# Expert stages in parts of 12 and 4 token tiles, causal query blocks first to last, four operand steps inside the passes

## The reference, cut to what matters

```python
# small-head attention, 16 heads of 8; full in the first layer, causal in the second
q = q * cos + _rotate_half(q) * sin ; k = k * cos + _rotate_half(k) * sin
scores = einsum('bqhd,bkhd->bhqk', q, k) / sqrt(D) ; causal mask in layer 2
y = softmax(scores) @ v ; x = x + y @ proj_w
# experts: layer 1 has 8 experts, top 2, and a shared one; layer 2 has 4 experts, top 1
logits = h @ router_w
out += gate[:, e] * (silu(h @ w_gate[e]) * (h @ w_up[e])) @ w_down[e]
```

## Time and profile before

| | us |
|---|---|
| median of 3 runs | 2046.22 |
| the profiled execution's span | 2040.1 |
| what lies around the span | 6.1 |
| PE busy | 1822.2 |
| DVE busy | 1547.6 |
| ACT busy | 1380.9 |
| POOL busy | 415.4 |

### The profile page before, as it was taken

How to read it: one execution, slowest core, us unless ns; L and a number is a source line. 1 busy time by engine, 2 the same in 40 slices (tenths; PEclk the granted TensorE clock), 3 DMA queues, 4 the chain that set the end, 5 groups by cost and what they waited for, 6 DMA issues and landing times. The chain is left out here.

```text
span 2040.1 us, 39849 instructions
## 1 busy us (share of the span) xinstructions
PE 1822.2 (89%) x15560; PEld 907.5 (44%) x15560; DVE 1547.6 (76%) x2263; ACT 1380.9 (68%) x2565; POOL 415.4 (20%) x650
## 2 busy tenths in 40 slices
PE   6699999999999798489989999999778999999784
PEld 2122222222223388435667776767512322233384
DVE  5899999999997443446767777877578979886434
ACT  3499999999999643255645656566347898888331
POOL 4201000000002324323432121221330101123413
PEclk8699999999999998889999999999867999999598
DMA  5000000000000378400000000000100000000274
GB/s 168 1 3 3 5 10 4 5 9 5 8 7 7 107 264 284 124 0 1 1 1 1 1 1 1 1 1 1 53 1 2 5 3 12 5 12 6 60 262 154
DMA packets 52874, 81.51 MB, mean 40 GB/s; under 512 B 9200, under 2 KB 37744, under 8 KB 52560
## 3 DMA queue, kind: packets, MB, share of 16 engines
q1 hardware_dynamic: 47520, 70.50, 10.9%
q0 software_dynamic: 3072, 6.30, 1.0%
q10 hardware_dynamic: 2096, 2.17, 0.4%
HBM read 64.13 MB, written 12.06 MB: 37 GB/s over the span
## 5 line engine op out<-in xcount | busy, mean ns | idle before, releaser
L826 DVE TENSOR_REDUCE a_mx<-psum 128x2 f32<-128x1024 f32 (+2 forms) x832 | 906.1, 1156 | 73.2 <-PE psum L601 40.2
L752 ACT ACTIVATE a_cs<-psum 128x512 f32<-128x512 f32 (+3 forms) x1664 | 857.0, 572 | 80.7 <-PE psum L619 62.4
L642 PE MATMUL psum<-a_cs,a_V 128*16 128x256 f32 (+1 forms) x6400 | 501.7, 384 | 20.9 <-ACT a_OD L732 9.7
L601 PE MATMUL psum<-a_KS,a_QS 48*128 48x512 bf16 (+3 forms) x1664 | 324.9, 381 | 32.9 <-DVE a_mx L826 29.7
L619 PE MATMUL psum<-a_QS,a_KS 51*128 51x512 bf16 (+3 forms) x1664 | 336.6, 378 | 4.9 <-ACT a_cs L752 3.1
L2122 PE MATMUL psum<-b_VW,b_ST 128*128 128x129 f32 x2176 | 252.5, 277 | 13.3 <-DVE X L2232 13.3
L2122 PEld LDWEIGHTS psum<-b_VW,b_ST 128*128 128x128 f32 x2176 | 248.5, 194 | 15.0 <-DVE X L2232 15.0
L619 PEld LDWEIGHTS psum<-a_QS,a_KS 51*128 51x128 bf16 x1664 | 87.7, 93 | 355.0 <-ACT a_cs L752 310.3
L2103 PE MATMUL psum<-b_GT,AT 128*128 128x512 f32 (+3 forms) x640 | 242.9, 534 | 1.6 <-ACT b_ST L2158 1.6
L642 PEld LDWEIGHTS psum<-a_cs,a_V 128*16 128x16 f32 x6400 | 107.1, 94 | 244.7 <-issue 120.2
L2207 DVE TENSOR_TENSOR b_M<-b_M,b_ST 128x512 f32<-128x512 f32 (+3 forms) x288 | 174.8, 607 | 43.1 <-ACT b_ST L2158 12.6
(11 more groups left out here) (225 smaller groups left out, 1514.5 us busy)
## 6 DMA issues: line engine op xcount, KB each, us to landing
e_W<-in_l_experts SPq DMA_DIRECT2D x45, 576.0 KB, 5.5
e_W<-in_l_experts SPq DMA_DIRECT2D x21, 768.0 KB, 5.8
yg<-e_yout SPq DMA_DIRECT2D x14, 256.0 KB, 6.0
xg<-zeros SPq DMA_DIRECT2D x2, 1472.0 KB, 9.8
a_cs<-in_rope ACTq DMA_DIRECT2D x4, 512.0 KB, 9.5
a_QS<-a_mrow SPq DMA_DIRECT2D x128, 3.0 KB
a_cs<-in_rope SPq DMA_DIRECT2D x1, 2048.0 KB, 7.8
a_num<-a_OD SPq DMA_DIRECT2D x120, 16.0 KB
```

The source lines that it names most:

```text
L601: mm = pe.matmul(ps[:, 2 * slot + half, 0:width], QS[rows, 2 * p + i, q_cols(qb, qt * P, P)], KS[rows, 2 * p + i, c * BLK:c * BLK + width] ...
L642: mm = pe.matmul(ps[32 * j:32 * j + 2 * HD, AV_BANK, a:b], V[:, kt, HPP * p + j, :], probs(e, a, b), start=(kt == 0 and half == 0), stop=last,
L752: act.activation(probs(HPP * s + j, c, BLK), ps[:, plan.bank(entry), c:BLK], ACT.Exp, scale=scale).then_inc(exp_done, 1)
L826: dve.tensor_reduce(mx[:, pk % 2, qt, 2 * i:2 * i + 2, c], banks, AX.X, ALU.max).then_inc(max_done, 1)
```

## The change

In both expert layers the parts become 12 and 4 tiles: 31 and 15 slots in the first layer, 15 and 7 in the second. Three blocks are early in both. In the first layer 16 of part 0's 24 scatters stay in the attention block, in the second 4 of 12; half of the rest are issued first in the expert block, half after the power of the late block's norm. Blocks whose gathered results don't fit into part 1's slots are collected, measured and normalized behind the last slot (`uncollected`, `unmeasured`, `closing`).

In the causal attention the query blocks go 0, 1, 2, 3, and the operands in the order k0 q0 k1 q1 k2 q2 k3 q3. Four stay in the lead; k2, q2, k3, q3 begin at halves 20, 44, 80 and 112 of the passes (`begun`). There their placement goes by four pairs through the two-slot ring and VectorE makes all four copies; ROTATE, REST, LOW, HIGH, MIDDLE and PLACE are their offsets in halves. The lead keeps 19 maxima (45 before) and two turned rows (one before). The second half of the cos and sin table is loaded into other memory, since the first table's memory holds the exponentials.

```diff
-        self.operands = [("k", 0), ("q", order[0])] + [("k", n) for n in range(1, NB)] + [("q", n) for n in order[1:]]
+        self.operands = []
+        for qb in order:
+            fresh = [("k", n) for n in range(self.chunks(qb)) if ("k", n) not in self.operands]
+            self.operands += fresh[:1] + [("q", qb)] + fresh[1:]
+        self.leading = len(self.operands) - len(begun)
+        self.begun = {self.leading + i: u for i, u in enumerate(begun)}
...
+        for s, u in self.begun.items():
+            for j in range(2):
+                self.halves[u + j].append(("project", s, j))
+            for v in range(NU):
+                self.halves[u + self.PLACE + 2 * v].append(("place", s, v))
...
     def by_vector(self, s, v):
-        return s < EARLY and v % 2 == 1
+        return s >= self.leading or s < EARLY and v % 2 == 1
...
-                front.scatter(pool, 0)
+                front.scatter(pool, 0, 0, front.SENT_EARLY)
...
+                def place_pair(s, v):
+
+                    which = 0 if plan.operands[s][0] == "k" else 1
+                    slot = slot_of(("place", s, v))
+                    if v == 0:
+                        pe.wait_ge(low, s + 1)
+                    for t in range(TERMS):
+                        for i in (2 * (v % 2), 2 * (v % 2) + 1):
+                            rows = slice(32 * i, 32 * (i + 1))
+                            mm = pe.matmul(ps[:, 2 * slot + i % 2, :], place[rows, which, t, SETS[v // 2][i], :],
+                                           terms[rows, s % 2, t, :], start=(t == 0), stop=(t == TERMS - 1))
+                    mm.then_inc(max_ready, 1)
...
-        self.blocks = [sorted(order[n:n + 2]) for n in range(0, NB, 2)]
+        self.blocks = [sorted(order[:split]), sorted(order[split:])]
...
+        if split == 3 and top2:
+            self.WHEN = {"project": (1, 2, 3), "turn": (10, 13, 16), "logits": (14, 17, 20), "exps": (21, 25), "count": 28,
+                         "chain": 30, "last": 30}
...
+            self.SENT_EARLY = 8
+        elif split == 3:
+            self.WHEN = {"project": (1, 2, 3), "turn": (10, 13, 16), "logits": (14, 17, 20), "exps": (), "count": 23,
+                         "chain": 25, "last": 25}
...
+            self.SENT_EARLY = 4
...
                 following.begin(pool)
+                left = len(plan.tiles[0]) - front.SENT_EARLY
+                front.scatter(pool, 0, front.SENT_EARLY, front.SENT_EARLY + left // 2)
                 for n in front.late:
                     front.power(pool, n)
+                front.scatter(pool, 0, front.SENT_EARLY + left // 2)
...
-                    for g in plan.blocks[b]:
+                    for g in (plan.measured, plan.unmeasured)[b]:
                         following.gpsimd(pool, g)
...
                 small_head_stage(core, "a1", AT, w, None, cs, arrived, KS, QS, V, place, kbias, AT, True,
-                                 forward[::-1], 13, None, None,
-                                 lambda sp: sp.dma_start(d1.table[:, :], a["table4"]).then_inc(d1.table_in, 16), front1)
+                                 forward, 11, None, None,
+                                 lambda sp: sp.dma_start(d1.table[:, :], a["table4"]).then_inc(d1.table_in, 16), front1,
+                                 (20, 44, 80, 112), late_cs)
```

More of the change, by code:

```diff
@@ L28 @@
 TPB = BLK // P
[L29 to L30 removed]
+PARTS = 2
+TABLE_TILES = 12
 HEADS, HD = 16, 8
@@ L137, in __init__ @@
             self.due.append((s, min(upto[pk] + TURN_AFTER, len(self.items))))
+        self.due = [(max(s, 0), n) for s, n in self.due]
         self.due[0] = (-1, upto[0] + beyond)
-        ahead = self.items[:self.sent(-1)]
-        self.first_turn = upto[0] + (TURN_AFTER if beyond >= TURN_AFTER else 0)
-        if beyond >= TURN_AFTER:
-            ahead.insert(self.first_turn, ("turn", 0))
-        else:
-            ahead.append(("turn", 0))
+        ahead = [x for item in self.items[:self.sent(-1)] for x in (item, behind.get(item)) if x]
+        self.lead_turns = sum(item[0] == "turn" for item in ahead)
         self.lead = self.lay(ahead)
@@ L157, in __init__ @@
                 self.ring += mine
-        self.ring += [item for row in self.halves for item in row if item[0] == "scores"]
+        self.ring += [item for row in self.halves for item in row if item[0] != "turn"]
         self.number = {}
@@ L177, in lay @@
     def lay(self, ahead):
-        lead = [[] for _ in self.operands]
+        lead = [[] for _ in range(self.leading)]
         left = list(ahead)
@@ L184, in lay @@
                 left.remove(item)
+        if self.leading < 4 + self.chunks(self.order[0]):
+            lead[-1] += left
+            return lead
         half = (len(left) + 1) // 2
-        lead[2 + NB] += left[:half]
-        lead[3 + NB] += left[half:]
+        lead[-2] += left[:half]
+        lead[-1] += left[half:]
         return lead
@@ L236, in max_step, with splits @@
         return rows[-1] // 2 if rows else -1
+    def splits(self, kind, u):
+        return [s for s, first in self.begun.items() if first + kind == u]
     def first_col(self, s):
@@ L251, in small_head_stage @@
 def small_head_stage(core, tag, src_T, w, bias, cs, arrived, KS, QS, V, place, kbias, OT, causal, order, beyond,
-                     tokens, opening, later, front):
+                     tokens, opening, later, front, begun=(), late_cs=None):
     nc, ps = core.nc, core.psum
     scale = float(HD) ** -0.5
-    plan = Plan(causal, order, beyond)
-    NS, NPK, NOP = len(plan.steps), len(plan.packs), len(plan.operands)
+    plan = Plan(causal, order, beyond, begun)
+    NS, NPK, NOP, NL, LT = len(plan.steps), len(plan.packs), len(plan.operands), plan.leading, plan.lead_turns
     H2 = BLK // 2
@@ L1761, in _ @@
                     if j == 0 and not shared:
-                        front.normalize(dve, front.late[1])
+                        for n in front.late[1:]:
+                            front.normalize(dve, n)
                     for _ in range(front.PIECES.get(j, 0)):
```

184 lines of the change are left out of this document (127 added, 57 removed).

## The result

The changed kernel takes **2063.8 us** (median of 4 runs) against 2046.6 us for the kernel before: ratio 1.0092, interval 1.0079 to 1.0105. It is slower by 0.9%; 2017 us had been forecast. The profiled executions differ a little more (spans 2061.7 and 2040.1 us), and they are what the stages are read from.

A forecast was written before the change was run, and what follows sets the result against it. PE and DVE were taken as nearly full in the causal passes, neither in the lead, with one hole per expert layer. 2040.1 - 5 - 46 + 24.5 - 4 + 1.5 = 2011.1, forecast as 2017 us; range 1996 to 2042.

The forecast's parts named there:

- causal lead: Stretch before the causal passes: four of eight operand steps and 19 of 45 maxima stay, -46 us (-50 to -38).
- causal passes: Causal attention's packs: moved steps and maxima summed by the larger engine per pack, 397 us for 372.7, +24.5 (+8 to +78).
- second experts: Second expert block: later opening +13.4, hole gone -8.3, one late block less -1.3, end +2; sum +1.5 us (-4 to +8).
- natural times: Causal packs' lengths before the inserted work, by query block: 9.3, 18.0, 27.1 and 35.9 us.
- Rival C: Causal passes: coupling through the two ring slots; +78 us if nothing overlaps, slower from +53 on; 2071 us, 9%.
- rival A: Causal passes: the inserted work fits into the slack, passes +8; 1999 us, 12%.
- Rival B: Causal passes: block 0's packs run at 1.2 GHz behind a half-clock lead, +27 us; 2044 us, 7%.
- The hole: First experts, slots 21 to 24: PE's wait while part 1's rows wait for scatters goes away, -10.8 us.
- -3 for one block less of variance and norm: First experts, slots behind part 1's beginning: one block's variance and norm instead of two, -3 us.
- The opening: First experts' start: first weights issued about 16 us after the barrier, behind rows behind scatters, +4 us.
- Rival D: Openings of both expert blocks cost more, weights behind rows behind scatters, +13 us in all; 2030 us, 12%.
- those 8 fewer gathers just pay for it: 0: First experts' end: 8 fewer last gathers (10 us) offset VectorE's 12 us stall in slot 44; 0, bounds -4 and +4.

The follow-up runs named there:

- first filler kernel: Changed kernel with each score matmul of the diagonal steps of the last two packs issued once more at full width: 2061.3 us, ratio 1.0086 to the kernel before.
- the kernel with fillers: Changed kernel with all operand steps in the lead, weights first, and score matmuls of packs 0 to 2 issued once more: 2044.9 us, ratio 1.0023.
- the kernel with one term: Changed kernel with one of three terms placed in each of the sixteen inserted placements, 32 matmuls instead of 96: 2055.3 us, ratio 1.0044.
- the two experiments on it: Changed kernel with the sixteen inserted copies on ScalarE instead of VectorE, 2060.6 us; changed kernel with a third of the inserted placements' matmuls, 2055.3 us.

## Why the prediction was wrong, step by step

| term | forecast | measured |
|---|---|---|
| first attention, later barrier | +5 | +4.2, and 2.4 of chance |
| first experts, from its barrier on | -10 | +0.6 |
| big-head stage | 0 | -4.8, chance |
| causal lead | -46 | -46.9 |
| causal passes | +24.5 | +68.3 |
| tail | -4 | -3.9 |
| second experts | +1.5 | +1.7 |

**The passes are the step that failed.** "Taking the larger of each, with half to one us for coupling" gave 46.5, 87, 119 and 142.7 us for the four blocks; measured were 57.8, 104.1, 125.4 and 153.1. The forecast noticed that VectorE and PE were each at 94 to 96% in a full pack and then let the new pieces of one run beside those of the other. In pack 4 the engines' sums were nearly right (DVE 22.5 us, 21.3 forecast), but the pack took 24.5: the coupling was 2 us, and 1 to 4 in packs 4 to 9, where 1 at most was allowed. A doubled placement costs 1.1 to 1.4 us of pack, about its VectorE copy of 1.28; taken from VectorE it gave almost nothing back, and taking two thirds of its matmuls gave about half of their time. In these packs an added piece was paid at about the length of its longer half, though neither engine was busy all the time.

Block 0 is over by 11.3 us, and that is another failure than coupling in full packs. Pack 0 took 19.3 us with PE busy for 16.7 of it at a clock of 0.58; pack 1, with as many maxima (14 in both), took 14.2. By these two packs the low clock cost pack 0 at most some 5 us, an estimate. The first pack of the kernel before, which also begins at half clock, takes 41.6 us with 35 maxima where the second takes 35.9 with 32; the forecast's natural times have no term for such a beginning.

The 68.3 us split like this. Order and 26 more maxima: 22.9. Four steps at full clock, by packs 4 to 9 at clocks of 1.00 in whichever profile shows them (packs 5 and 6 in that of the first filler kernel: 24.05 and 25.48) against the kernel with all steps in the lead: 6.4 + 6.0 + 2.6 + 3.8 + 5.1 + 4.9 = 28.8, and 4.1 in block 0, together 33. The other 12.4 is clock: 6.3 in packs 14 and 15, 6.1 in packs 5 and 6. So a step costs 8.2 us inside where it cost 7.05 outside, and a maximum 0.88 for 0.72, if all of the two differences is put down to maxima and none to the order. **By these profiles the move had no gain to give even without the falls of the clock from pack 5 on**: 56 us in for 47 out, and 3.9 more out in the tail. Rival C, coupling, came nearest, and its point of turning (+53) was passed, but its full form (nothing overlaps, +78) did not come. It had been given 9% because maxima and scores overlap in the packs of before, which says nothing on what happens to the next piece when both engines are over 90%. Of the forecast's +24.5 and its upper bound of 78, the bound was the nearer.

Some terms under the sum don't come out of the forecast's own rows. Two projections of 1.12 us are 2.2 us and not 1.8, and the passes show 2.25. A placement pair was put at 0.65 us; in pack 4 it takes 0.82, as long as a set of twelve. Together PE has 5.5 us to do for a step and not 4.4. Block 0's 46.5 is at least 1.3 us more than its listed sums with 1 us of coupling each, and rival A's 1999 should be 2001 by its own passes of +8. None of this turns the sum.

**Rival B, the half clock, was half right.** Packs 0 to 2 did run at 0.58, 0.87 and 0.79. In pack 0 that cost up to 5 us (above); in packs 1 and 2, little as far as the kernel with fillers shows. The sign "clock near 1.0 from the second pack on" did not come, and the dearer falls were not forecast at all: those in wide packs. In the five traces with query blocks 3 to 0, each of packs 1 to 10 is the same within 0.02 us and ran at 1.00, while pack 11 fell to 0.91 in two of them. Of the thirteen traces with blocks 0 to 3, ten have a pack from 5 on below 0.97, at 0.5 to 9 us each (the last pack of the kernel with one term took 45.9 us, 37.0 at full clock in others); the three without such a fall all have their steps in the lead. Pack 14 or 15 fell in nine. Of the rule weighed ahead, that the default is the slow clock and activity lifts it (the Trainium skill, TensorE: Matmul & The Clock Gate, section "Part 1: The HAM clock gate"), packs 1 and 2 with filler are a case that agrees, and so is the lead filled with float32 matmuls (0.89 for 0.80); the lead filled with bf16 ones is one that does not (0.75). The same page of the Trainium skill (section "A second HAM failure mode: psum-queue depth-cycling") tells of short idle times between groups of matmuls over cycling PSUM banks that make the clock swing; the traces agree only as far as the clock does swing in packs 5 to 11, whose matmuls go through the ring's banks; no run here shows the idle times to be the cause. The same pack is at 1.00 in one trace and at 0.72 in the next, and what decides that stays open.

**The lead** came at 40.8 us, -46.9 for -46. What the forecast did not ask is what lay under its cover: ten maxima there were free.

**First experts.** The hole did go (slot 21 to slot 24 took 7.6 us for 17.2, -9.6; -10.8 forecast). The -3 for one block less of variance and norm did not come: slot 24 to slot 45 took 49.7 us for 50.0. From slot 2 to slot 45 it is 101.0 us for 112.6, where the two terms had promised -13.8. The opening was mis-sized: +7.9 us to slot 2, where 4 had been allowed. The first weights were issued at 724.67, 16.3 us after the barrier as computed, but slot 1 began 9.1 us after that. SyncE stood 3.6 us in this issue (0.34 in each of the four behind it, 1.5 in the first of the kernel before), and the last load of rows, issued ahead of it at 723.06, landed only at 732.25; which of the two held the first weights up the trace doesn't tell. Slot 1 then ran at half clock (2.90 us for 1.50). Rival D was this, for one of its two openings. VectorE's stall was computed as 12 us and came as 10.4. But "those 8 fewer gathers just pay for it: 0" was wrong: from the last up matmul to the barrier 42.8 us for 38.4, so +4.4, just over the upper bound. Both were removable, by 6.8 and 7.5 us.

**Tail and second experts** came as forecast, slot 1 at 21.9 us after the barrier (21.5 forecast) and the stage at 108.2. In the tail there is luck in it: its selection matmuls took 3.6 us, at half clock, where the forecast had them at full clock. In the profile with all steps in the lead they took 1.9 and the tail 6.4 us, -5.7. The threshold given ahead, passes over 425 us, named the failure.

What stays open: how much of the loss in packs 4 to 9 is each side of the ring's (the two experiments on it contradict each other, and the waits go over from one side to the other when a side is relieved), how much of the 22.9 us is the order and how much the maxima, and what makes the clock fall in one execution and not in the next.

## What to carry to other kernels

Before work is moved from a stretch that waits into one that is 94% busy on two coupled engines, price each added piece at the full duration of its longer half (1.1 to 1.4 us here for 1.28), and ask what it hides where it stands; a waiting engine in an operand chain may be hiding it for nothing. When a queue's item is moved ahead of or behind others, ask what each one behind it waits for: the two repairs here (weights ahead of rows that wait, a short power ahead of the last third of the gathers) turned a part split that gained nothing into a kernel 0.7% faster, some 9 us of it in the stages they touch, while the same move in the block where nothing waited cost 11.6 us.

## What the hardware showed that had not been expected

- The same instructions take 581.8 to 589.0 us in the untouched big-head stage, over the kernels here. The kernels in the new order with all steps in the lead and their repairs ranged over 21 and 23 us in twelve executions each, the kernel before over 8 to 15 in 17 to 20.
- A float32 matmul of 128 x 512 stands in the trace as two and cost 0.98 us; the bf16 one of 48 x 512 0.31 at the lead's mixed clock.
- 48 bf16 filler matmuls (14.9 us busy) did not hold the clock in the lead (0.75, without them 0.80), 48 float32 ones (46.8 us) had it at 0.89, and 16 more a pack held it at 1.00 in packs 1 and 2 (without them 0.86 and 0.75).
- Two ScalarE copies of 128x1024 in a placement set took 1.94 us, so four operand copies are 3.9 us of chain; VectorE's is 1.28.
